# Selective scan with grouped exponentials: a ring of three decay tiles, three rotating sum tiles, and earlier broadcast rows

## The reference, cut to what matters

```
# experts (every expert is computed, weights of the unused are zero)
h   = gelu(einsum('te,ieh->tih', xf, w1) + b1)
out = sum((einsum('tih,ihe->tie', h, w2) + b2) * weights[..., None], axis=1)
x   = x + gb * out
# scan
x_val = silu(conv4(x @ W_in_x)) ; z = x @ W_in_z
dt    = softplus(x[:, :, :64] @ W_dt.T + b_dt) ; Bm = x @ W_B.T ; Cm = x @ W_C.T
dA    = exp(dt_t[:, :, None] * A[None])            # 16 states x 256 channels
h     = dA * h + (dt_t * xv_t)[:, :, None] * B_t[:, None, :]
y_t   = einsum('bdn,bn->bd', h, C_t)
y     = (y * silu(z)) @ W_out.T
# Fourier layer: a linear map of the next layer norm, plus bias
```

## Time and profile before

| | us |
|---|---|
| three runs | 614.37, 614.96, 619.1 (median 614.96) |
| the profiled execution | 613.03 |
| its span, first to last instruction | 611.0 |
| busy PE / DVE / ACT / POOL | 480.0 / 430.9 / 363.4 / 314.4 |
| mean granted TensorE clock | 0.944 |

### The profile page before, as it was taken

One profiled execution on the slowest core, in us unless ns is written; L12 is line 12 of the kernel. 1 busy time (PEld: TensorE's weight loads), 2 busy tenths in 40 slices (PEclk: granted clock), 3 DMA queues, 4 the chain that ended last, 5 costly groups with the idle time before them and its releaser, 6 DMA issues.

```text
span 611.0 us, 6868 instructions
## 1 busy us (share of the span) xinstructions
PE 480.0 (79%) x2346; PEld 335.5 (55%) x2346; DVE 430.9 (71%) x723; ACT 363.4 (59%) x507; POOL 314.4 (51%) x220
## 2 busy tenths in 40 slices
PE   3768867579899999988879898799896198477763
PEld 3455535344678887676757587666775033133222
DVE  4768898954542441269977989888899628989961
ACT  0533341225665575699999998899998138523301
POOL 3226986757201101235776567776587527647541
PEclk9979999989999999999999989999899589988786
DMA  8600000000000000404756626757527403112000
GB/s 307 253 1 0 1 1 1 1 0 0 1 1 1 2 1 3 137 1 109 188 117 169 139 75 167 161 117 195 131 59 179 97 0 105 65 39 86 0 0 17
DMA packets 15009, 44.74 MB, mean 73 GB/s; under 512 B 2240, under 2 KB 7744, under 8 KB 12544
## 3 DMA queue, kind: packets, MB, share of 16 engines
q0 software_dynamic: 2448, 17.83, 14.4%
q1 hardware_dynamic: 11952, 25.57, 12.4%
q10 hardware_dynamic: 576, 0.92, 0.4%
HBM read 25.31 MB, written 1.18 MB: 43 GB/s over the span
## 4 chain that ended last, share of the span: by engine, by line
PE 18%; ACT 15%; DVE 13%; issue 7%; POOL 5%; DMA 3%; POOLq 0%; ACTq 0%; DVEq 0%
DVE Hs L767 7%; DVE pCT L754 4%; ACT dA L991 4%; PE pO L1237 3%; ACT gel L979 3%; DMA Acc<-ZS 3%; ACT L991 3%; PE pY L1325 2%; PE pY L1278 2%; POOL ZS L388 2%; PE pH L1225 2%; ACT L979 2%; PE pH L1278 2%; ACT ln_x L841 2%; PE pH L1227 1%
## 5 line engine op out<-in xcount | busy, mean ns | idle before, releaser
L1237 PEld LDWEIGHTS pO<-w_e,gel 128*128 128x128 f32 x1024 | 125.5, 196 | 17.4 <-issue 8.8
L1237 PE MATMUL pO<-w_e,gel 128*128 128x128 f32 x1024 | 128.3, 280 | 4.3 <-DVE X L738 3.8
L767 DVE TENSOR_TENSOR_SCAN Hs<-dA,HL,pCT 128x512 f32<-128x512 f32 x96 | 117.7, 1267 | 4.0 <-POOL Zev L388 2.4
L754 DVE TENSOR_TENSOR pCT<-u,pB 128x1024 f32<-128x1024 f32 x64 | 78.4, 1225 | 42.5 <-PE pB L1303 41.5
L979 ACT ACTIVATE gel<-pH,b_e 128x512 f32<-128x512 f32 x128 | 86.0, 687 | 30.5 <-PE pH L1227 29.7
L388 POOL TENSOR_TENSOR ZS<-Hs,Crow 128x1024 f32<-128x1024 f32 x32 | 75.9, 2376 | 51.0 <-DVE Hs L767 51.0
L991 ACT ACTIVATE dA<-dt,a_neg 128x512 f32<-128x512 f32 x128 | 81.9, 711 | 28.1 <-DVE Hs L767 27.8
L388 POOL TENSOR_TENSOR Zev<-Hs,Crow 128x1024 f32<-128x1024 f32 x26 | 63.7, 2452 | 28.6 <-DVE Hs L767 21.4
L1225 PE MATMUL pH<-h2h,w_e1h 128*128 128x512 f32 x128 | 57.8, 452 | 22.0 <-ACT gel L979 20.8
L738 DVE SCALAR_TENSOR_TENSOR X<-pO,wts,X 128x128 f32<-128x128 f32 x128 | 35.8, 342 | 35.5 <-PE pO L1237 35.4
L444 POOL TENSOR_TENSOR ZA<-Qsb,S 128x1024 f32<-128x1024 f32 x16 | 38.0, 2376 | 32.0 <-DVE S L662 31.0
(11 more groups left out here) (227 smaller groups left out, 875.5 us busy)
## 6 DMA issues: line engine op xcount, KB each, us to landing
Crow<-c_rows SPq DMA_DIRECT2D x32, 512.0 KB, 4.0
Acc<-ZS POOLq DMA_DIRECT2D x10, 1024.0 KB, 8.7
Acc<-Zev POOLq DMA_DIRECT2D x7, 1024.0 KB, 7.0
w_e<-in_w_e SPq DMA_DIRECT2D x2, 2048.0 KB, 10.6
X<-in_x SPq DMA_DIRECT2D x4, 256.0 KB, 6.9
out<-h2T SPq DMA_DIRECT2D x4, 256.0 KB, 3.8
S<-in_w_mod ACTq DMA_DIRECT2D x2, 384.0 KB, 4.7
w_cx<-in_conv_row SPq DMA_DIRECT2D x1, 512.0 KB, 9.3
```

Of the source, the lines that this page charges most:

```text
L754: vec.tensor_tensor(pU[:, :, 0:w], half_of(u, c), pB[:, None, 0:w].to_broadcast([P, ND, w]), ALU.mult).then_inc(s["mam_ub"], 1)
L767: vec.tensor_tensor_scan(Hs[:, 2 * o + d, 0:w], dA[:, 4 * (p % 2) + 2 * o + d, 0:w], pU[:, d, 0:w], HL[:, d, n:n + 1] if c else 0.0, ALU.m ...
L1237: ins = mm(pO[:, j * P:(j + 1) * P], gel[:, n % NG, j * P:(j + 1) * P], w_e2[:, NK * (g % E) + k, :], start=(k == 0 and j == 0), stop=(k = ...
```

## The change: what it does

- **ACT.** In every odd pair p the exponentials of pairs p+1 and p+2 are computed, eight in a row; in even pairs none. dA becomes a ring of three pairs' tiles, and the wait for the scans is moved to match (`decays(q)` waits for the scans of pair q-3).
- **Sums.** Acc, Zev and ZS (four tiles' worth) become one tensor Zt of three: odd pairs take tile 1; even pairs and the accumulator share tiles 0 and 2, which swap with the chunk. A pair from ALONE on takes a whole tile by its parity, so `output(20, 0)` waits for the DMA of pair 18 alone, and the accumulated part is added on PE in `total(21)` instead of `total(20)`.
- **PE order.** `row_b(2p+2)` comes ahead of the "A" stages where there are experts and an "A" stage on PE (k = 2, 5, 6, 7), stays behind `down` 0 and 1 where there is none, and comes right after "A" (ahead of `total` and "B") where there are no experts. `fft` moves from place "A" to place "B" of k = 4, on PE and on DVE.
- h5T goes; the Fourier layer's input uses the tile h4T.

```diff
--- before.py
+++ after.py
@@ -155,10 +155,9 @@
         pr = sb("pr", [P, NJ, E])
         s4 = sb("s4", [P, 3, NJ])
         rank = sb("rank", [P, NJ, E])
-        dA = sb("dA", [P, 2 * 2 * ND, TC])
+        dA = sb("dA", [P, 3 * 2 * ND, TC])
         Hs = sb("Hs", [P, 2 * ND, TC])
-        Zev = sb("Zev", [P, 2 * ND, TC])
-        ZS = sb("ZS", [P, 2 * ND, TC])
+        Zt = sb("Zt", [P, 3, 2 * ND, TC])
         Crow = sb("Crow", [P, 2 * NCB, TC])
         BCf = sb("BCf", [96, 2, TC])
         y2 = sb("y2", [P, ND, TC])
@@ -224,6 +221,17 @@
         def summed(c):
 
             return NP * (c + 1) <= ALONE
+
+        def acc_of(c):
+
+            return Zt[:, 2 * (c % 2), :, 0:WIDTHS[c]]
+
+        def z_of(p):
+
+            c, k = divmod(p, NP)
+            if k == 0 and not alone(p):
+                return acc_of(c)
+            return Zt[:, 1 if k % 2 else 2 - 2 * (min(c, ALONE // NP) % 2), :, 0:WIDTHS[c]]
 
         def sums(p):
 
@@ -265,7 +273,7 @@
                 if 0 <= tail:
                     plan += [(1, "mid", "gate", tail), (2, "A", "project", tail), (2, "end", "tail_x", tail),
                              (2, "end", "ln_stats", tail), (3, "apply", "ln_apply", tail), (3, "C", "ln_turn", tail, 2),
-                             (3, "end", "bias", tail), (4, "A", "fft", tail)]
+                             (3, "end", "bias", tail), (4, "B", "fft", tail)]
                 if 0 <= front < NL:
                     plan += [(4, "mid", "ln_stats", front), (4, "apply", "ln_apply", front), (4, "C", "ln_turn", front, 1),
                              (5, "A", "x_part", front, 0), (5, "B", "rows", front), (6, "A", "x_part", front, 1),
@@ -365,23 +373,14 @@
 
                 m, w = 2 * p + o, WIDTHS[p // NP]
                 c, k = divmod(p, NP)
-                h = slice(2 * (p % 2), 2 * (p % 2) + 2)
                 part = slice(2 * o, 2 * o + 2)
-                if alone(p):
-                    Z = [Zev, ZS][o][:, h, 0:w]
-                    if p >= ALONE + 2:
-                        pool.wait_ge(s["mam_y"], totals(p - 2))
-                    elif p == ALONE and o == 0:
-                        for q in (p - 2, p - 1):
-                            pool.wait_ge(mam_s[q % 2], 16 * sums(q))
-                elif k == 0:
-                    Z = Acc[:, c % 2, part, 0:w]
-                    if c >= 2:
-                        pool.wait_ge(s["mam_y2"], 2 * (c - 1))
-                else:
-                    Z = [Zev, ZS][p % 2][:, part, 0:w]
-                    if p >= 2 and o == 0 and sums(p - 2):
-                        pool.wait_ge(mam_s[p % 2], 16 * sums(p - 2))
+                Z = z_of(p)[:, part, :]
+                if p >= ALONE + 2:
+                    pool.wait_ge(s["mam_y"], totals(p - 2))
+                elif p >= 2 and o == 0 and sums(p - 2):
+                    pool.wait_ge(mam_s[p % 2], 16 * sums(p - 2))
+                if k == 2 and c and p < ALONE + 2 and o == 0:
+                    pool.wait_ge(s["mam_y2"], 2 * c)
                 if o == 0:
                     pool.wait_ge(mam_c[p % NCB], 16 * (p // NCB + 1))
                 pool.wait_ge(s["mam_sc"], 2 * m + 2)
@@ -399,7 +398,7 @@
                 pool.wait_ge(s["mam_z"], 2 * p + 2)
                 if sums(p - 1):
                     pool.wait_ge(mam_s[(p - 1) % 2], 16 * sums(p - 1))
-                pool.dma_start(Acc[:, c % 2, :, 0:w], [Zev, ZS][p % 2][:, :, 0:w], accum_op=ALU.add).then_inc(mam_s[p % 2], 16)
+                pool.dma_start(acc_of(c), z_of(p), accum_op=ALU.add).then_inc(mam_s[p % 2], 16)
 
             link(pool.memset(mhalf[:, :], -0.5))
             pool.memset(ones[:, :], 1.0).then_inc(s["set_pool"], 1)
@@ -984,16 +983,16 @@
                 c, k = divmod(p, NP)
                 if k == 0:
                     act.wait_ge(s["mam_dt"], 2 * c + 2)
-                if p >= 2:
-                    act.wait_ge(s["mam_sc"], 4 * (p - 1))
+                if p >= 3:
+                    act.wait_ge(s["mam_sc"], 4 * (p - 2))
                 for r in range(4):
                     n = 2 * k + r // 2
-                    nc.scalar.activation(dA[:, 4 * (p % 2) + r, 0:WIDTHS[c]], half_of(dt, c)[:, r % 2, :], ACT.Exp,
+                    nc.scalar.activation(dA[:, 4 * (p % 3) + r, 0:WIDTHS[c]], half_of(dt, c)[:, r % 2, :], ACT.Exp,
                                          scale=a_neg[:, r % 2, n:n + 1]).then_inc(s["mam_dA"], 1)
 
             def turned(c, which, b):
 
-                ln([h2T, h4T, h5T][which][:, 0:WIDTHS[c]], c, 2 + 2 * which, b, None if which else h2h[:, c, 0:WIDTHS[c]])
+                ln([h2T, h4T, h4T][which][:, 0:WIDTHS[c]], c, 2 + 2 * which, b, None if which else h2h[:, c, 0:WIDTHS[c]])
 
             def run(p, stages, places):
 
@@ -1009,8 +1008,9 @@
             for p, stages in later_stages():
                 if 0 <= p + AHEAD < NL * E:
                     hidden(p + AHEAD, range(NK))
-                if 0 <= p + 1 < NL * NP:
-                    decays(p + 1)
+                for q in (p + 1, p + 2) if p % 2 else ():
+                    if 0 <= q < NL * NP:
+                        decays(q)
                 run(p, stages, "AB")
                 run(p, stages, ("apply",))
                 run(p, stages, "C")
@@ -1250,18 +1250,20 @@
                 if moe:
                     up(g, 2)
                     up(g, 3)
+                early = not moe or any(at == "A" and stage in mine for at, stage, *_ in stages)
+                if moe and early and 0 <= 2 * p + 2 < NL * NS:
+                    row_b(2 * p + 2)
                 run(p, stages, "A")
+                if not moe and 0 <= 2 * p + 2 < NL * NS:
+                    row_b(2 * p + 2)
                 if 0 < p < NL * NP:
                     total(p - 1)
-                if not moe:
-                    run(p, stages, "B")
                 if moe:
                     down(g, 0)
                     down(g, 1)
-                if 0 <= 2 * p + 2 < NL * NS:
+                if not early and 0 <= 2 * p + 2 < NL * NS:
                     row_b(2 * p + 2)
-                if moe:
-                    run(p, stages, "B")
+                run(p, stages, "B")
                 if moe:
                     down(g, 2)
                     down(g, 3)
@@ -1309,21 +1311,23 @@
                 c, k = divmod(p, NP)
                 if k == 0 and c:
                     pe.wait_ge(s["mam_y2"], 2 * c)
-                h, w = 2 * (p % 2), WIDTHS[c]
+                w = WIDTHS[c]
                 if p == ALONE:
                     use(2, "mam_y", 1)
                     use(3, "mam_y", 1)
-                if p == ALONE and k:
-                    for q in (p - 2, p - 1):
+                first = k == 0 or p == ALONE
+                Z = z_of(p)
+                for o in range(2):
+                    pe.wait_ge(s["mam_z"], 2 * p + o + 1)
+                    for d in range(ND):
+                        ins = mm(pY[d][:, 0:w], ident[:, :], Z[:, 2 * o + d, :], start=(first and o == 0),
+                                 stop=(k == NP - 1 and o == 1))
+                if p == ALONE + 1 and k > 1:
+                    for q in (p - 3, p - 2):
                         pe.wait_ge(mam_s[q % 2], 16 * sums(q))
                     for d in range(ND):
                         for o in range(2):
-                            mm(pY[d][:, 0:w], ident[:, :], Acc[:, c % 2, 2 * o + d, 0:w], start=(o == 0), stop=False)
-                for o, Z in ((0, Zev), (1, ZS)):
-                    pe.wait_ge(s["mam_z"], 2 * p + o + 1)
-                    for d in range(ND):
-                        ins = mm(pY[d][:, 0:w], ident[:, :], Z[:, h + d, 0:w], start=(k == 0 and o == 0),
-                                 stop=(k == NP - 1 and o == 1))
+                            ins = mm(pY[d][:, 0:w], ident[:, :], acc_of(c)[:, 2 * o + d, :], start=False, stop=False)
                 ins.then_inc(s["mam_y"], 1)
 
             def project(c, b):
```

More of the change, by code:

```diff
@@ L172, in build @@
         HL = sb("HL", [P, ND, NS])
-        Acc = sb("Acc", [P, 2, 2 * ND, TC])
-        h5T = sb("h5T", [P, TC])
         outb = h2T[:, :].rearrange("p (j d) -> p j d", j=NJ)
@@ L498, in gate @@
                     pool.wait_ge(s["mam_o"], c)
-                pool.tensor_tensor(Acc[:, c % 2, 0:2, 0:w], Acc[:, c % 2, 0:2, 0:w], Acc[:, c % 2, 2:4, 0:w],
+                pool.tensor_tensor(acc_of(c)[:, 0:2, :], acc_of(c)[:, 0:2, :], acc_of(c)[:, 2:4, :],
                                    ALU.add).then_inc(s["mam_zs"], 1)
@@ L503, in gate @@
                 for d in range(ND):
-                    pool.tensor_tensor(y2[:, d, 0:w], Acc[:, c % 2, d, 0:w], half_of(gz, c)[:, d, :],
+                    pool.tensor_tensor(y2[:, d, 0:w], acc_of(c)[:, d, :], half_of(gz, c)[:, d, :],
                                        ALU.mult).then_inc(s["mam_y2"], 1)
@@ L766, in scans @@
                 for d in range(ND):
-                    vec.tensor_tensor_scan(Hs[:, 2 * o + d, 0:w], dA[:, 4 * (p % 2) + 2 * o + d, 0:w], pU[:, d, 0:w],
```

(3 more changed lines are left out.)

## The result

The changed kernel takes 626.94 us (median of 4 runs, 624.59 to 628.76) against 614.97 us (4 runs) for the kernel before in the same session: a ratio of 1.018, with a 95% interval from 1.012 to 1.024. It is slower; I had forecast 611.4. The profiled execution took 624.59 us, its span is 622.6 us, and its mean granted clock is 0.927 (before: 613.03, 611.0 and 0.944).

A forecast was written before the change was run, and what follows sets the result against it. DVE was taken to set the time in pairs 1 to 4, ACT and PE being full in pairs 5 and 6. Terms 4 + 6 - 10.5 - 3 = -3.5 us gave 611.4 against the median 614.96, range 599 to 622.

The forecast's parts named there:

- Part 1, table loads: ACT loses 20 table loads, 26 us of its busy time; worth nothing where DVE runs without a gap.
- Part 2, uneven exponentials: Eight exponentials in odd pairs make the ACT-PE loop 17.4 to 17.5 us per two pairs against DVE's 17.1.
- Part 3, pairs 5 to 16: Pairs 5 to 8 and 13 to 16: DVE's wait moves, little lost; with the uneven exponentials +4 us, bounds -9 and +13.
- Part 4, PE's clock: PE's longer idle gaps in six even pairs lower its clock: 1.3 us a gap, +6 us, bounds 0 and +19.
- Part 5, pairs 20 to 23: No POOL wait for pair 19's DMA and earlier B rows: -10.5 us at `products(48)`, bounds -5.5 and -14.
- part 6: Pairs 24 to 31: `row_b(52)` issued ahead of `total(24)` removes a 2.64 us wait; -3 us taken, bounds 0 and -4.
- The clock falls in each even pair: Rival: PE's clock stays down through `up` and `down`, deciding above 1.9 us a gap; 624.5 us at its bound, chance 0.14.
- Full clock: Rival: the new idle gaps of PE leave its clock up; sum -9.5, 605.4 us, chance 0.20.
- Loads pay: Rival: ACT's and PE's lead absorbs the unevenness and early rows fill DVE; sum -17.5, 597.5 us, chance 0.14.
- Transition worth little: Rival: the POOL wait moves to pair 21, so pairs 20 to 23 give only -3; 619 us, chance 0.10.

The follow-up runs named there:

- e7: The change without its grouped exponentials, and with gelu replaced by tanh in the experts (not the reference's result): 599.60 us, 0.975 of the kernel before.
- e12: The changed kernel plus extra unused matmuls on PE in seven even pairs, three in 2, 4, 10, 18 and two in 0, 8, 16: 616.32 us, ratio 1.001.
- e2: The changed kernel without the grouped exponentials, new sum tiles and PE order kept: 606.46 us, 0.985 of the kernel before.
- e6: The changed kernel with the old exponentials, and the early B row only where no experts run: 605.07 us, 0.982 of the kernel before.
- e1: The kernel before with only the three rotating sum tiles added: 610.79 us, 0.991 of the kernel before.
- e9: The changed kernel, grouping kept, with gelu replaced by tanh in the experts (not the reference's result): 602.84 us, 0.977 of the kernel before.
- e8: The changed kernel without the grouped exponentials, plus four extra matmuls on PE at the end of pair 20: 606.72 us, 0.986 of the kernel before.

## Why the prediction was wrong

*Part 1, table loads: right.* ACT has 487 instructions where it had 507, the 20 loads. e7 confirms that they are worth nothing where DVE runs without a gap.

*Part 2, uneven exponentials: right in kind.* The loop at full clock takes 17.7 us for two pairs (e12) where I had 17.4 to 17.5, and ACT idles in the even pair. The start cost was 2.8 us by my stepping and 2.5 in e12 against e2. One sign failed: I had `moe_acc` still 8.5 to 9 us apart in pairs 1 to 4, and two pairs took 20.16 us, 10.1 each; 17.69 at full clock (e12).

*Part 3, pairs 5 to 16: too small.* Parts 2 and 3 together were +4. With the gaps filled (e12) the stretch from `step` to `products(40)` takes 221.1 us against 211.8 before: +9.3, inside the bound of +13. Two terms were mis-sized. I gave `fft` out of pair 12 a net gain of 1.3 us, but the layer norm of that chunk stands behind the eight exponentials of pair 11, and that stretch is 3.0 us longer in e12 than in e2. And for pairs 9 to 18 together I had a loss of 0.7, where e12 against e2 shows 3.1 in pairs 13 to 16 alone. Both figures hold some clock, as the rows of e12 at 394.76 and 445.31 show. That the early rows beside experts earn nothing was right (e6).

*Part 4, PE's clock: the step that failed.* The gaps were forecast at 3.6 to 4.6 us and are 3.31 to 4.34 in the six pairs; the mechanism was named; the price was 1.3 us "for a gap, less where DVE has slack", 6 in all. PE's timeline in pairs 10 and 16 shows how a gap is priced:

```profile
380.61 0.50 PE L1225 MATMUL pH<-h2h,w_e1h 128*128 128x512 f32 x1 [3.31 <-ACT gel L978]
380.95 0.39 PE L1226 MATMUL pH<-h2l,w_e1h 128*128 128x512 f32 x1
...
381.69 0.63 PE L1226 MATMUL pH<-h2l,w_e1h 128*128 128x512 f32 x1
...
385.74 2.51 PE L1237 MATMUL pO<-w_e,gel 128*128 128x128 f32 x21
...
453.92 0.79 PE L1225 MATMUL pH<-h2h,w_e1h 128*128 128x512 f32 x1 [4.34 <-ACT gel L978]
...
460.06 0.41 PE L1305 MATMUL pB<-ST,sel 96*128 96x512 bf16 x1
```

From the end of the gap to the B row it is 6.14 us in pair 16 (453.92 to 460.06), for what takes 3.28 at full clock: 2.86 lost. In pair 10 it is 5.13 us to the next `down` (380.61 to 385.74), for 1.50 + 0.22 + 1.78 = 3.50: 1.63 lost. Pairs 2, 4, 8 and 18 lost 2.47, 2.61, 1.35 and 2.85 in the same way, in all 13.8 us for six, a mean of 2.3. Pair 0, which I had not counted, adds 1.60. That agrees with the 14.1 us between the change and e12 in the stretch to `products(40)`, and with the 10.6 between their medians. My 1.3 was chosen between 0 and 3.2 by the nearest rows, and I weighed them wrongly: I let 1.91 us of idle time that had cost nothing speak against the window in which the clock fell to 0.66, though the new gaps are twice as long. All seven new gaps before a second `up` brought it down. I had also counted on slack of DVE, but in pairs 1 to 4 there is none.

The Trainium skill, "TensorE: Matmul & The Clock Gate", section "HAM oscillation — how this bites in real kernels", warns of a PE that waits between bursts and falls to the lower clock at each. These runs agree: seven gaps of 3.3 to 4.3 us, seven falls. The Trainium skill, "ScalarE: Activation LUTs", section "Table sets: the hidden batching unit", advises to batch activations by table set. Here this removed 20 loads of 1.28 us and made the kernel 20.5 us slower.

*Part 5, pairs 20 to 23, right in the sum; part 6 at its bound.* Forecast -13.5 from `products(40)` on; measured -11.4. The sum tiles alone gave 6.6 of this (135.6 us in e1 against 142.2), where the POOL wait was priced at 5.5. Up to `products(48)` it is -11.1 (468.80 to 522.02 before, 491.76 to 533.90 after) against my -10.5; part 6's -3 came out as -0.3, at its bound of 0. The close sum of part 5 is in part luck: up to `products(44)` the gain is 16.1 us (34.65 before, 18.53 after) where I had 13 to 14, and then 5.0 come back where I had some 3, because I had left out POOL's `rows` operations.

*The rivals.* "The clock falls in each even pair" is what happened; it decided as said, since a gap costs 2.3 us and its point was 1.9 (by the sum's own terms, 4 + 6 gaps - 13.5, the sign turns at 1.6). Its time, 624.5 us for a median, was worked out from part 4's upper bound of +19 with +4 for the order. The 626.94 is made of less clock and more order: in the profiled stretch +14.1 and +9.3, then -11.4 behind pair 20, -0.5 for the earlier start. "Full clock" fell with the windows. "Loads pay" fell with e7: 6.9 us is the worth of 43 loads, not of 20. "Transition worth little" fell with part 5. In the sum, part 4 was off by 8 us, parts 2 and 3 by 5, and parts 5 and 6 by 2. Parts 2 to 4 lay inside their bounds, and the error of part 4 alone, added to 611.4, would have stayed in the range (619.5). Together with parts 2 and 3 it doesn't (624.8): I had made the range as if only one of them could be off, though both come from the same bunching.

What stays open: how the at most 9.9 us of the order of work split between the late layer norm, the late evacuations of pairs 8 and 16 and what is left of the fallen clock in e12, since no kernel moves one of them alone. No run has a third bank between PE and ACT either, so that two are too few is read from the loop and not shown.

## What to carry to other kernels

Removed overhead on an engine is worth only what the engine can use: here the loop of two engines that hand tiles to each other through two banks went through the longest uninterrupted block on one of them, so grouping work to save setup time lengthened the loop even as it shortened the sum. Before bunching, put the block beside the buffer depth, and charge TensorE's idle time behind it at the price of the work that follows it at the lower clock (here 1.3 to 2.9 us a gap), not at zero. And a change of several parts is to be read part by part: here two parts gained 1.5% while the third lost 3.4%.

## What the runs showed of the hardware

- Beside the experts, idle gaps of PE of 3.3 to 4.5 us were each followed by matmuls at the lower level (0.63 instead of 0.39 us, 16 `down` matmuls in up to 3.60 instead of 1.95), for 1.3 to 2.9 us of lost time in the seven ahead of an `up`. Shorter gaps went both ways: one of 1.91 us cost nothing, one of 2.00 us in e9 brought the clock down.
- The fall doesn't always come with the first matmul behind the gap: at 380.61 in the change three ran at full speed and the next ones didn't.
- Matmuls without use paid for themselves in gaps that PE had anyway: 18 of them (e12) took 10.6 us off the median. Four ahead of `x_part` (e8) raised the clock, ran at the lower one themselves (4.53 us), and took nothing off.
- Table loads took 1.28 us each, and the operation behind one began 10 to 20 ns after it (288.92 to 290.21 above).
